# Gate product moved ahead of the inner products and the states in each slot of a state-space loop

## The chip, the core and the metric
The kernel runs on one core of one Trainium2 chip. The metric is the device time of one execution in microseconds (us). All times of the profile are from one profiled execution of the kernel before, counted from the start of its span.

## What is computed
Four layers one after the other on an input of 2 x 512 x 512: an attention layer, a gated feed-forward layer, a state-space layer (Mamba-2 style) and a grouped feed-forward layer, each with layer norms and a residual sum. The change is in the state-space layer, which works on 2 sequences of 512 positions, 128 heads of 64, in 8 groups of 16 heads, with chunks of 128 positions:

```python
proj = jnp.einsum('bsd,ed->bse', x, in_proj_w)
gate, hBC, dt = ...
hBC = jax.nn.silu(causal_conv4(hBC))            # per channel, 4 taps
Y_diag = einsum('bzlhn,bzshn,bhzls,bzshp->bzlhp', Cc, Bc, L, xch)    # inside a chunk
states = einsum('bzlhn,bhzl,bzlhp->bzhpn', Bc, decay_states, xch)    # a chunk's end state
Y_off  = einsum('bzlhn,bzhpn,bhzl->bzlhp', Cc, prev, exp(A_cum))     # from earlier chunks
y = Y_diag + Y_off + hs * D
g = y * jax.nn.silu(gate)
out = rmsnorm_per_group(g) * norm_w
return einsum('bsi,oi->bso', out, out_proj_w)
```

## The kernel before
The large products are in fp32r: each operand is cut into a high and a low part and three products are summed (`product`, L96 to L98), so 12 matmuls of 512 columns make one product over 512 inputs.

The state-space stage runs over 8 groups `g`, 2 sequences `b`, and `CT` = 10 slots `k` for each pair of these: 16 half-groups of 10 slots, and a tail. In the text, slot 7 means a slot with `k == 7`, and T7 the moment in which TensorE starts its conv product. The first two columns of a half-group are B and C, the other eight (`GT` = 8) are pairs of heads. A slot is a software pipeline: each engine has its own program of all slots, written out in order, and `behind(g, b, k, lag)` says which item a step with this lag works on (or none). What each engine does in a slot:

- TensorE (`on_tensor`): `projection` (the conv product, 12 matmuls), `inside` (lag 5, the products inside chunks, L1301), `states` (lag 5, L1310), `gate` (lag 3, the gate product, 12 matmuls), `project` (lag 8, output projection, 12 matmuls, L1331 to L1333), `before` (lag 6, the part of earlier chunks, L1344), in slot 6 `squares`, then `turn` (lag 4, transposes, L1356). Because of the lags, slots 3 and 4 have no `inside` and `states`, slots 1 and 2 no `gate`, slots 6 and 7 no `project`, slots 4 and 5 no `before`.
- VectorE (`on_vector`): first tap of the conv (`tap` 0), `with_dt` (xdt, L1521, waits for `turn` of the slot ahead), tap 1, `offset` (L1540), tap 2, `mixing` of one head (mix, L1547), `skip` (y, L1566, waits for `inside` of this slot), in slot 8 `accumulate` 0 and 1 (x, L1603), `carry` (state, L1572 and L1580, waits for `states` of this slot), `mixing` of the other head, in slot 8 `accumulate` 2 and 3, `low` (y_lo, L1588), and in the first sequence's half-groups `cut_out` (w_o_lo, L1593), once or twice a slot from slot 3 to slot 8. The three taps read the result of the last slot's conv product out of PSUM.
- ScalarE (`on_scalar`): weight cuts, the conv's first read (`first_tap`), SiLUs, `gate` (sg, L1451, which empties the gate product's bank), and the decays of mix. GpSimd (`on_pool`): `to_end` (xend), `finish` (y), low parts of weights, squares. SyncE issues all DMAs.

Two PSUM banks serve conv and gate products by turns, `k % 2` for the conv product and the other for the gate product. So the gate product of slot `k` overwrites the conv product of slot `k - 1`, and waits until its taps are done; the next conv product waits until ScalarE has emptied the gate's bank. One bank (`SPARE_D`) serves `inside` and `before` by turns, one (`SPARE_C`) `states` and `turn`, so that `before` and `turn` wait for `skip` and `carry` of the same slot:

```python
def gate(bb, i):
    wait(pe, "taps_done", g, b, (K1 - 1) * k if main else 0)
def before(bb, i):
    if i < GT - 1:
        wait(pe, "skip_done", g, bb, i + 2)
def turn(bb, i):
        wait(pe, "state_done", g, bb, 2 * i)
def project(bb, i):
        if i == 0:
            wait(pe, "acc_done", g, bb, z + 1 - ZB)
```

The last one holds in slot 8, where `project` starts a new accumulation in the four output banks that `accumulate` of the same slot empties.

Of the kernel before, what the change touches and what calls it, by code (L numbers as in the profile page):

```python
# [92 lines left out]
def product(pe, out, terms):  # L93

    for n, (a_hi, a_lo, b_hi, b_lo) in enumerate(terms):
        pe.matmul(out, a_hi, b_hi, start=(n == 0), stop=False)  # L96
        pe.matmul(out, a_hi, b_lo, start=False, stop=False)  # L97
        last = pe.matmul(out, a_lo, b_hi, start=False, stop=(n == len(terms) - 1))  # L98
    return last
# [800 lines left out]
def state_space(core, w_conv_in, w_gate_in, w_dt, w_out1, chan_wb, dt_bias, a_log, norm_w, c_keep):  # L900
# [8 lines left out]
    with ExitStack() as outer:  # L909
# [195 lines left out]
        with ExitStack() as inner:  # L1105
# [63 lines left out]
            def wait(eng, name, g, b, j):  # L1169

                value = (g * B + b) * PER[name] + j
                if value > 0:
                    eng.wait_ge(s[name], value)

            def behind(g, b, k, lag):

                i = k - lag
                if i >= 0:
                    return (b, i) if i < GT and g < G1 else (b, None)
                if g == 0 and b == 0:  # L1180
                    return b, None
                return (b - 1, i + CT) if i + CT < GT else (b - 1, None)
# [90 lines left out]
            def on_tensor(pe, g, b, k):  # L1273
# [3 lines left out]
                def projection():  # L1277
                    n = (b * CT + k) % RING
                    wait(pe, "win_low", g, b, k + 1)
                    wait(pe, "taps_done", g, b, (K1 - 1) * (k - 1))  # L1280
                    bb, i = behind(g, b, k, 4)
                    if i is not None:
                        wait(pe, "gate_done", g, bb, i + 1)
                    at = slice(b * S, (b + 1) * S)
                    last = product(pe, ps[:, k % 2, :], [
                        (w_in_hi[:, n, c, :], w_in_lo[:, n, c, :], xt_hi[:, c, at], xt_lo[:, c, at]) for c in range(KD)])
                    last.then_inc(s["proj_ready"], 1)
# [17 lines left out]
                def states(bb, i):  # L1305

                    wait(pe, "bt_done", g, bb, 1)
                    wait(pe, "xend_done", g, bb, i + 1)
                    for z in range(ZB - 1):
                        last = pe.matmul(ps[:, SPARE_C, cols(z)], bt[:, z, :], xend[:, i % 2, z, :], start=True, stop=True)  # L1310
                    last.then_inc(s["st_ready"], 1)

                def gate(bb, i):

                    wait(pe, "wg_low", g, bb, i + 1)
                    wait(pe, "taps_done", g, b, (K1 - 1) * k if main else 0)
                    at = slice(bb % B * S, (bb % B + 1) * S)
                    last = product(pe, ps[:, 1 - k % 2, :], [
                        (w_g_hi[:, i % RING, c, :], w_g_lo[:, i % RING, c, :], xt_hi[:, c, at], xt_lo[:, c, at]) for c in range(KD)])
                    last.then_inc(s["gate_ready"], 1)  # L1320
# [63 lines left out]

                if main:
                    projection()
                bb, i = behind(g, b, k, 5)
                if i is not None:
                    inside(bb, i)
                    states(bb, i)  # L1390
                bb, i = behind(g, b, k, 3)
                if i is not None:
                    gate(bb, i)
                bb, i = behind(g, b, k, 8)
                if i is not None:
                    project(bb, i)
                bb, i = behind(g, b, k, 6)
# [4 lines left out]
                bb, i = behind(g, b, k, 4)  # L1402
# [323 lines left out]
            with nc.Block() as blk:  # L1726
                @blk.sync
                def _(sp):
                    sp.dma_start(keep_ls[:, :], c_keep).then_inc(s["const_loaded"], 16)
                    groups(sp, loads)  # L1730

                @blk.tensor
                def _(pe):
                    pe.wait_ge(s["ones_set"], 1)
                    groups(pe, on_tensor)

                @blk.scalar
                def _(act):
                    groups(act, on_scalar)

                @blk.vector
                def _(dve):
                    dve.wait_ge(s["const_loaded"], 16)
                    groups(dve, on_vector)

                @blk.gpsimd
                def _(pool):
                    pool.memset(ones[:, :], 1.0).then_inc(s["ones_set"], 1)
                    pool.memset(acc[:, :, :], 0.0).then_inc(s["acc_zero"], 1)
                    groups(pool, on_pool)  # L1750
# [427 lines left out]
```

## Time and profile before
| | |
|---|---|
| time, median of 3 runs | 2871.81 us (2871.59 to 2872.53) |
| profiled execution: its time, its span | 2870.13 us, 2868.3 us |
| TensorE matmul busy over the span | 2618.6 us, 91% |
| VectorE, ScalarE, GpSimd busy over the span | 59%, 49%, 51% |
| mean granted TensorE clock | 0.964 |
| a light slot 8 (1667.64 to 1679.19), a heavy one (1771.73 to 1784.26) | 11.55 us, 12.53 us |
| TensorE busy in 1200 to 2600 us | 193 to 194 us in each 200 us |

The state-space loop runs from about 1090 us to about 2750 us. Its half-groups differ little from each other: two of them (one for each sequence) take 204.9 to 206.7 us in the steady part. Slots take 8.5 to 12.5 us. In the rows below, the half-group whose slot 0 starts at 1690.49 belongs to the first sequence (with `cut_out`, "heavy" in the text), the one ahead of it to the second ("light").

### The profile page before, as it was taken

What the parts mean: (1) busy time and instruction counts of PE and PEld (TensorE: products, weight loads), DVE (VectorE), ACT (ScalarE), POOL (GpSimd) and SP (SyncE); (2) the same over time, 40 slices, a digit from 0 to 9 for tenths busy, and PEclk for the clock granted to TensorE, in tenths of its full rate; (3) what the DMA queues carried; (4) which work ended last, traced back from release to release, by engine and by line L of the source; (5) the groups of instructions that cost most, each with busy time, mean ns of one, the idle gap of its engine ahead of it and who ended that gap; (6) DMA issues with size and microseconds to landing.
All of it is one profiled execution on the core that took longest, in us unless ns stands there. A gap on an engine that the chain in (4) does not pass through costs nothing. (4 is left out here: it accounts for less than half of the span.)

```text
span 2868.3 us, 37544 instructions
## 1 busy us (share of the span) xinstructions
PE 2618.6 (91%) x12920; PEld 1874.7 (65%) x12920; DVE 1680.8 (59%) x3054; ACT 1398.2 (49%) x2762; POOL 1457.5 (51%) x1267
## 2 busy tenths in 40 slices
PE   7999999799979936999999999999999999999948
PEld 3464444444458724787887887877877877877734
DVE  2131211366542464777777787678678778778765
ACT  2100000355322116677668668667766766866703
POOL 0042222344300103776776776786776776777651
PEclk9999999899989958999999999999999999999978
DMA  5000200000021015334334334333433333334210
GB/s 207 0 12 0 88 0 0 30 1 1 1 88 37 1 53 176 111 93 155 94 95 147 110 104 125 109 111 116 127 103 118 115 111 111 115 112 124 75 47 30
DMA packets 137292, 233.36 MB, mean 81 GB/s; under 512 B 27408, under 2 KB 47632, under 8 KB 136848
## 3 DMA queue, kind: packets, MB, share of 16 engines
q1 hardware_dynamic: 137104, 230.96, 25.7%
q8 instruction: 105, 1.72, 0.3%
q14 instruction: 83, 0.68, 0.1%
HBM read 223.57 MB, written 7.34 MB: 81 GB/s over the span
## 5 line engine op out<-in xcount | busy, mean ns | idle before, releaser
L428 PE MATMUL ps<-w,q 128*128 128x512 f32 x768 | 332.3, 592 | 1.5 <-DVE raw L449 1.5
L1459 ACT ACTIVATE mix<-mix,sc 128x128 f32<-128x128 f32 x1024 | 310.8, 389 | 3.4 <-DMA mix<-row_cum 3.3
L96 PE MATMUL ps<-s_xt_hi,w_in_hi 128*128 128x512 f32 x640 | 266.3, 416 | 49.0 <-ACT sg L1451 32.8
L1558 DVE SCALAR_TENSOR_TENSOR feat<-ps,chan,feat 128x511 f32<-128x511 f32 (+2 forms) x384 | 283.7, 739 | 10.4 <-ACT feat L1441 8.7
L1670 POOL TENSOR_TENSOR w_in_lo<-w_in_raw,w_in_hi 128x512 fp32r<-128x512 f32 x160 | 216.1, 1351 | 115.4 <-ACT w_in_hi L1416 115.4
L1547 DVE TENSOR_TENSOR mix<-mix,cb 128x512 f32<-128x512 f32 x256 | 271.7, 1066 | 0.0
L428 PEld LDWEIGHTS ps<-w,q 128*128 128x128 f32 x768 | 145.8, 190 | 185.1 <-issue 183.2
L1588 DVE TENSOR_TENSOR y_lo<-y,y_hi 128x512 fp32r<-128x512 f32 x128 | 171.0, 1336 | 161.0 <-ACT y_hi L1475 159.3
L98 PE MATMUL ps<-s_xt_hi,w_in_lo 128*128 128x512 f32 x640 | 252.4, 394 | 0.0
L97 PE MATMUL ps<-s_xt_lo,w_in_hi 128*128 128x512 f32 x640 | 251.1, 392 | 0.0
L1654 POOL TENSOR_TENSOR xend<-xdt,sc 128x384 f32<-128x384 f32 x128 | 106.8, 834 | 281.3 <-DVE xdt L1521 279.6
L96 PE MATMUL ps<-s_xt_hi,w_g_hi 128*128 128x512 f32 x512 | 213.2, 416 | 21.1 <-DVE feat L1558 21.0
L1331 PE MATMUL ps<-w_o_hi,y_hi 128*128 128x512 f32 x512 | 207.4, 405 | 5.4 <-DVE y_lo L1588 3.4
L502 POOL TENSOR_TENSOR sq<-raw 128x512 f32<-128x512 f32 (+1 forms) x24 | 23.2, 967 | 357.1 <-DVE raw L449 357.1
L98 PE MATMUL ps<-s_xt_hi,w_g_lo 128*128 128x512 f32 x512 | 204.0, 398 | 0.0
L1333 PE MATMUL ps<-w_o_hi,y_lo 128*128 128x512 f32 x512 | 203.3, 397 | 0.0
L1332 PE MATMUL ps<-w_o_lo,y_hi 128*128 128x512 f32 x512 | 203.1, 397 | 0.0
L97 PE MATMUL ps<-s_xt_lo,w_g_hi 128*128 128x512 f32 x512 | 201.5, 394 | 0.0
L1666 POOL TENSOR_TENSOR y<-y,sg 128x512 f32<-128x512 f32 x128 | 195.1, 1524 | 10.0
L1675 POOL TENSOR_TENSOR w_g_lo<-w_g_raw,w_g_hi 128x512 fp32r<-128x512 f32 x128 | 200.1, 1563 | 0.0
L653 ACT ACTIVATE qt<-ps 128x512 f32<-128x512 f32 x16 | 9.4, 665 | 381.6 <-PE ps L581 381.6
L1441 ACT ACTIVATE feat<-ps,chan 128x512 f32<-128x512 f32 x128 | 98.4, 769 | 180.6 <-PE ps L98 180.6
(246 smaller groups left out, 6006.3 us busy)
## 6 DMA issues: line engine op xcount, KB each, us to landing
mix<-row_cum SPq DMA_DIRECT2D x128, 512.0 KB, 5.7
w_in_raw<-in_w_conv_in SPq DMA_DIRECT2D x160, 256.0 KB, 3.3
w_g_raw<-in_w_gate_in SPq DMA_DIRECT2D x128, 256.0 KB, 3.4
ecb<-row_ecum SPq DMA_DIRECT2D x256, 96.0 KB, 3.4
w_o_raw<-in_w_out SPq DMA_DIRECT2D x64, 256.0 KB, 3.0
w<-in_w_c2q SPq DMA_DIRECT2D x16, 768.0 KB, 7.7
wqkv<-in_w_qkv SPq DMA_DIRECT2D x1, 3072.0 KB, 13.7
f_w_int<-in_w_gate SPq DMA_DIRECT2D x11, 256.0 KB, 2.6
```

The costliest lines, as they stand in the source:

```text
L96: pe.matmul(out, a_hi, b_hi, start=(n == 0), stop=False)
L97: pe.matmul(out, a_hi, b_lo, start=False, stop=False)
L98: last = pe.matmul(out, a_lo, b_hi, start=False, stop=(n == len(terms) - 1))
L428: mm = pe.matmul(dst, src[:, c, b, z * P + tap:(z + 1) * P + tap], w, start=(c == 0 and tap == 0), stop=False)
L1331: pe.matmul(ps[:, OUT + z, :], a_hi, w_o_hi[:, i, :], start=(i == 0), stop=False)
L1332: pe.matmul(ps[:, OUT + z, :], a_hi, w_o_lo[:, i, :], start=False, stop=False)
L1333: last = pe.matmul(ps[:, OUT + z, :], a_lo, w_o_hi[:, i, :], start=False, stop=(i == GT - 1))
L1459: last = act.activation(m, m, ACT.Relu, bias=sc[:, b, CUM, z, 2 * i + e:2 * i + e + 1], scale=-1.0)
L1547: last = dve.tensor_tensor(m, m, cb[:, :], ALU.mult)
L1558: dve.scalar_tensor_tensor(out=to, in0=ps[:, j % 2, 0:S - back], scalar=chan[:, bb % B, j, K1 - 1 - back:K1 - back], in1=to, op0=ALU.mult, ...
L1670: pool.tensor_tensor(w_in_lo[:, n % RING, :, :], w_in_raw[:, n % RING, :, :], w_in_hi[:, n % RING, :, :].bitcast(F32), ALU.subtract).then_ ...
L1675: pool.tensor_tensor(w_g_lo[:, i % RING, :, :], w_g_raw[:, i % RING, :, :], w_g_hi[:, i % RING, :, :].bitcast(F32), ALU.subtract).then_inc ...
```

## The change
In every slot TensorE's program has `gate` directly behind `projection`, ahead of `inside` and `states`. No instruction is added or removed, no wait is added or dropped, and the programs of the four other queues are word for word the same.

```diff
                 if main:
                     projection()
+                bb, i = behind(g, b, k, 3)
+                if i is not None:
+                    gate(bb, i)
                 bb, i = behind(g, b, k, 5)
                 if i is not None:
                     inside(bb, i)
                     states(bb, i)
-                bb, i = behind(g, b, k, 3)
-                if i is not None:
-                    gate(bb, i)
                 bb, i = behind(g, b, k, 8)
                 if i is not None:
                     project(bb, i)
```

TensorE's rows in a slot 7, before: from the last matmul of the conv product (w_in) over `inside` (mix, xdt), `states` (xend, bt) and the gate product (w_g) to `before` (featc, state) and `turn` (ident).

```order
L98 MATMUL ps<-s_xt_hi,w_in_lo 128x512
L1301 MATMUL ps<-mix,xdt 64x128 x8
L1310 MATMUL ps<-xend,bt 128x128 x3
L96 MATMUL ps<-s_xt_hi,w_g_hi 128x512
...
L98 MATMUL ps<-s_xt_hi,w_g_lo 128x512
L1344 MATMUL ps<-featc,state 128x128 x3
L1356 MATMUL ps<-ident,feat 128x128 x4
```

The same slot of the changed kernel:

```order
L98 MATMUL ps<-s_xt_hi,w_in_lo 128x512
L96 MATMUL ps<-s_xt_hi,w_g_hi 128x512
...
L98 MATMUL ps<-s_xt_hi,w_g_lo 128x512
L1301 MATMUL ps<-mix,xdt 64x128 x8
L1310 MATMUL ps<-xend,bt 128x128 x3
L1344 MATMUL ps<-featc,state 128x128 x3
L1356 MATMUL ps<-ident,feat 128x128 x4
```

The twelve matmuls of the gate product no longer stand between `states` and `before`; these two, and `inside` and `before`, are now neighbours.

TensorE's rows in a slot 8, before, which has the output projection (w_o) too:

```order
L98 MATMUL ps<-s_xt_hi,w_in_lo 128x512
L1301 MATMUL ps<-mix,xdt 64x128 x8
L1310 MATMUL ps<-xend,bt 128x128 x3
L96 MATMUL ps<-s_xt_hi,w_g_hi 128x512
...
L98 MATMUL ps<-s_xt_hi,w_g_lo 128x512
L1331 MATMUL ps<-w_o_hi,y_hi 128x512
...
L1344 MATMUL ps<-featc,state 128x128 x3
```

And in the changed kernel:

```order
L98 MATMUL ps<-s_xt_hi,w_in_lo 128x512
L96 MATMUL ps<-s_xt_hi,w_g_hi 128x512
...
L98 MATMUL ps<-s_xt_hi,w_g_lo 128x512
L1301 MATMUL ps<-mix,xdt 64x128 x8
L1310 MATMUL ps<-xend,bt 128x128 x3
L1331 MATMUL ps<-w_o_hi,y_hi 128x512
...
L1344 MATMUL ps<-featc,state 128x128 x3
```

Here `inside` and `states` stand between the gate product and the output projection, and the gate product follows the conv product at once. The same exchange is made in slots 0, 5, 6, 7, 8 and 9; slots 1 to 4 keep their order, since they lack one of the two.

## Rows read from the trace of the kernel before

**Rows 1.** What TensorE waited for, 1200 to 2600 us: total, times, longest.

```profile
PE ps L96 <- DVE feat L1558: 20.7, 14, 2.7
PE ps L96 <- ACT sg L1451: 20.3, 21, 1.3
PE ps L1331 <- DVE x L1603: 1.7, 6, 0.3
```

**Rows 2.** Timeline of TensorE, slot 0: start, us, instruction, [idle before].

```profile
1690.49 0.47 PE L96 MATMUL ps<-s_xt_hi,w_in_hi 128*128 128x512 f32 x1
...
1693.43 1.10 PE L1301 MATMUL ps<-mix,xdt 128*64 128x128 f32 x16
...
1695.15 0.47 PE L96 MATMUL ps<-s_xt_hi,w_g_hi 128*128 128x512 f32 x1
...
1698.00 0.39 PE L1331 MATMUL ps<-w_o_hi,y_hi 128*128 128x512 f32 x1
...
1700.80 0.83 PE L1344 MATMUL ps<-featc,state 128*128 128x128 f32 x6
1701.46 0.60 PE L1356 MATMUL ps<-ident,feat 128*128 128x128 f32 x4
1701.82 0.48 PE L96 MATMUL ps<-s_xt_hi,w_in_hi 128*128 128x512 f32 x1
```

**Rows 3.** Timeline of VectorE, the same slot 0.

```profile
1690.78 0.69 DVE L1521 TENSOR_TENSOR xdt<-ps,sc 128x512 f32<-128x512 f32 x1 [2.52 <-PE ps L1356]
...
1692.50 0.74 DVE L1558 SCALAR_TENSOR_TENSOR feat<-ps,chan,feat 128x509 f32<-128x509 f32 x1
...
1694.58 0.75 DVE L1566 SCALAR_TENSOR_TENSOR y<-feat,chan,ps 128x512 f32<-128x512 f32 x1 [0.35 <-PE ps L1301]
...
1696.53 0.68 DVE L1547 TENSOR_TENSOR mix<-mix,cb 128x512 f32<-128x512 f32 x1
1697.13 1.53 DVE L1588 TENSOR_TENSOR y_lo<-y,y_hi 128x512 fp32r<-128x512 f32 x1
1698.58 0.74 DVE L1558 SCALAR_TENSOR_TENSOR featb<-ps,chan,featb 128x511 f32<-128x511 f32 x1
```

**Rows 4.** Timeline, slot 4 of a light half-group: last tap, gate product.

```profile
1631.40 0.73 DVE L1558 SCALAR_TENSOR_TENSOR feat<-ps,chan,feat 128x509 f32<-128x509 f32 x1
...
1632.28 0.47 PE L96 MATMUL ps<-s_xt_hi,w_g_hi 128*128 128x512 f32 x1 [0.28 <-DVE feat L1558]
```

**Rows 5.** Timeline of VectorE, light slots 7 and 8.

```profile
1664.30 1.70 DVE L1547 TENSOR_TENSOR mix<-mix,cb 128x512 f32<-128x512 f32 x1
1667.05 0.69 DVE L1588 TENSOR_TENSOR y_lo<-y,y_hi 128x512 fp32r<-128x512 f32 x1 [1.05 <-ACT y_hi L1475]
...
1672.35 1.40 DVE L1603 SCALAR_TENSOR_TENSOR x<-ps,rr,x 128x512 f32<-128x512 f32 x2
...
...
1675.87 1.40 DVE L1603 SCALAR_TENSOR_TENSOR x<-ps,rr,x 128x512 f32<-128x512 f32 x2
```

**Rows 6.** Timelines of ScalarE (slot 6) and TensorE (slots 7, 8), light.

```profile
1656.60 0.60 ACT L1451 ACTIVATE sg<-ps 128x512 f32<-128x512 f32 x1 [1.02 <-PE ps L98]
...
1666.45 0.60 PE L1356 MATMUL ps<-ident,feat 128*128 128x128 f32 x4
1667.64 0.47 PE L96 MATMUL ps<-s_xt_hi,w_in_hi 128*128 128x512 f32 x1 [0.60 <-ACT sg L1451]
```

**Rows 7.** Timeline, heavy slot 5: the last two taps, `inside`.

```profile
1744.30 1.51 DVE L1558 SCALAR_TENSOR_TENSOR feat<-ps,chan,feat 128x510 f32<-128x510 f32 x2
...
1744.65 1.09 PE L1301 MATMUL ps<-mix,xdt 128*64 128x128 f32 x16
```

**Rows 8.** Group of `cut_out`, 1200 to 2600 us: busy, mean ns, idle before.

```profile
L1593 DVE SCALAR_TENSOR_TENSOR w_o_lo<-w_o_raw,nw,w_o_hi 128x512 fp32r<-128x512 f32 x55 | 66.0, 1220 | 0.0
```

**Rows 9.** Windows over two heavy gate products: us, busy by engine, PEclk, DMA.

```profile
1735.70:1739.00 3.30, 3.27 (x14) 2.73 (x15) 3.15 (x3) 1.81 (x5) 3.22 (x3) 1.00 0.03 9
2147.30:2151.80 4.50, 4.45 (x13) 3.57 (x14) 4.35 (x4) 3.03 (x9) 4.42 (x4) 0.65 0.03 9
```

## The prediction
> **What bounds the kernel now.** I read the page first (TensorE 91% busy, the others near half), then the list of waits of the state-space loop, then the timelines of TensorE and VectorE slot by slot. In 1400 us of the loop TensorE waits about 43 us: 20.7 for taps, 20.3 for ScalarE's sg, 1.7 for the accumulations [rows 1]. So TensorE is the bound, and nothing done to the order of its work can give back more than these 3%. What counts is whether VectorE, which shares PSUM banks with it, still delivers in time once its partners on TensorE move.
>
> In a full slot TensorE issues without a gap [rows 2]. From T (start of the conv product): `inside` and `states` at +2.94, gate product +4.66, `project` +7.51, `before` +10.31, `turn` +10.97, next slot +11.33. So the pieces hold it 2.9 (conv or gate), 1.72, 2.80 (`project`), 0.66 and 0.36.
>
> VectorE in the same slot [rows 3]: xdt at +0.29 (0.29 behind the end of `turn`), last tap ending at +2.75, y at +4.09, which is 1.15 behind the start of `inside`; then, counted from y: the second mix at 1.95 (so `carry` is done near 2.05), y_lo at 2.55, next slot's first tap at 4.00, done at 4.74. That is +8.83, and xdt is due at 11.33 + 0.29 = 11.62: VectorE has 2.8 us to spare, seen as its 2.52 us wait for `turn`.
>
> **The change, part by part.** It adds and removes nothing. It starts the gate product 1.7 us earlier, and `inside`, `states` 2.9 later. Nothing else moves, DMA issues included.
>
> *The gate product's own wait.* It waits for the last tap of the same slot. In a slot 4, where nothing stands between the products, a tap that ended at 1632.13 let the gate go at 1632.28, 0.15 later [rows 4]. A punctual VectorE ends its taps at +2.75, so the gate can go at +2.90, as TensorE comes free. Cost 0 to 0.05 us, but the cover of 1.7 us is gone: from here on each microsecond of lateness of VectorE costs TensorE one.
>
> *VectorE's loop.* `inside` is now at +5.80, y at +6.95, taps done at 11.69, xdt due at 11.62. The spare 2.8 us are used up: in full slots (9 and 0) it fits to 0.1 us. In shorter slots and where VectorE has more to do it does not. Slot by slot, light half-groups first:
>
> - Slot 5: no `offset`, taps early. 0.
> - Slot 6: no `project` between `states` and `before` any more. `before` waits for y: 6.95 + 0.75 + 0.15 = +7.85 against +7.5. 0.35. `squares` covers the wait of `turn`.
> - Slot 7: the same 0.35; then `turn` waits for `carry`: 6.95 + 2.05 + 0.15 = +9.15 against 8.2 + 0.35 = 8.5, so 0.65 more. Its gate product meets taps 0.4 late, since slot 6 was 9.7 long and VectorE's loop 11.4 less what slot 7 leaves out. Given back: ScalarE's sg. It waited 1.02 us for the gate product of slot 6 and so came late in slot 7, where conv 8 waited for it: 1667.64 less 1666.45 + 0.36 is 0.83 [rows 6]. The gate product now is done before ScalarE comes to it, so this goes. Sum 0.35 + 0.65 + 0.4 - 0.83 = +0.6.
> - Slot 8: y of slot 7 is at T7 + 7.35, the second mix at 9.3. It took 1.70 in the old place, 0.68 in slot 0; y_lo 0.69 and 1.53 [rows 3, 5]. Where they fall beside GpSimd's work is not known; I take 1.1 and 1.0, between the bounds. With the first tap, xdt starts at T7 + 12.0. Slot 7 is now 9.9 long (8.5 + 1.0 + 0.4), so this is T8 + 2.05 and 1.75 late; the gate product is 1.7 late. Then `inside` at +7.5, y at 8.65, accumulations 0 and 1 from 9.3 to 10.7. `project` comes at +9.2 (7.5 + 1.7) and waits for accumulation 0 until 10.15 (0.95). Accumulations 2 and 3 start 3.52 behind 0 and 1 [rows 5], at 12.85, so `project`'s third bank, due at 11.55, waits until 13.65 (2.1). The old slot lost 0.25 here (of the 1.7 us of x [rows 1]). Sum 1.7 + 0.95 + 2.1 - 0.25 = 4.5.
> - Slots 9 and 0: 0.1 together.
>
> Light: 0.35 + 0.6 + 4.5 + 0.1 = 5.5 us.
>
> Heavy half-groups have w_o_lo besides, 1.22 us each [rows 8], one in each of slots 5 to 8 and two in slots 3 and 4. In slot 5 the last taps end at 1745.81, so the gate could go at 1745.96, while `inside` took over from conv at 1744.65 [rows 7]: 1.3, now paid in full. Slots 6 and 7: 0.5 each. Slot 8: xdt 1.2 later than in the light one, so gate 2.9 late, then 0.95 and 2.1, in all 5.9; the old heavy slot already lost 1.2 by the same late VectorE (12.53 against 11.33 for a full slot). 4.7. Slot 9: 0.3. Heavy: 7.3 us.
>
> Eight light half-groups give 44. Seven heavy ones give 51; the first half-group has no accumulation and is held by ScalarE, 0. Together 95 us.
>
> *TensorE's clock.* After a 2.7 us wait for taps in a heavy slot 4, one gate product ran at granted 1.00 and took 3.3 us, another at 0.65 and took 4.5 [rows 9]: part of the latter was at 1.2 instead of 2.4 GHz, 1.2 us dearer, for a like wait ahead of it. The Trainium skill (TensorE: Matmul & The Clock Gate, Part 1) has idleness bring the half rate; the trace agrees, with 0.65, though not each time. The new waits of slot 8 are of this size. I count 1.2 us in half of 15 slots 8: 9 us; bounds 0 and 2.4 x 15 = 36.
>
> Sum: 2870.1 (the profiled execution, 1.7 below the median) + 95 + 9 = **2974 us**, +3.6%, and 2976 by the median.
>
> **Rivals.**
>
> *Faster: VectorE keeps up in slot 8.* Then the change only removes ScalarE's waits: 0.83 in each light half-group and the like of it in heavy ones (20.3 us in seven pairs, of which slot 4's stay): 8 x 2 = 15 us, 2856. It decides at xdt of slot 8 starting by T8 + 0.4. For it: the sg wait that goes is real. Against it: even with both shared operations at their short 0.69, xdt comes at T7 + 11.2, which is T8 + 1.4. 4%. No measurable change, by such a balance: 3%.
>
> *Half the cost.* Second mix and y_lo take 0.69 wherever VectorE comes late, because GpSimd has by then finished. Then the light slot 8 costs 3.2, slots 6 and 7 nothing, heavy ones 4.5 in all: 8 x 3.2 + 7 x 4.5 = 57, 2927. For it: GpSimd runs while VectorE waits for `inside`. Against it: GpSimd's chain in slot 7 starts with xdt, which is late too. 15%.
>
> *VectorE becomes the bound in every slot from 5 to 0.* The loop fits full slots to 0.1 us only with y_lo and mix as in slot 0. If they take 1.53 and 1.70 there, the loop is 12.4 against 11.33 in two slots, and slots 7 and 8 are dearer by 1: some 3 us more in each half-group, 48, and the clock at its upper bound, 27 more: 2974 + 75 = 3049. For it: both long values are in the rows. Against it: the total work of VectorE is as before, and the collisions so far fall where GpSimd is busiest. Beside it, the Trainium skill (SBUF — State Buffer, Who interferes with whom) says that VectorE and GpSimd hold a shared port by turns, for a whole instruction. The trace agrees in the two lengths of y_lo, 0.69 and 1.53. 16%.
>
> **The numbers.** Main case 62%, its own range 2940 to 3010. Half cost 15%, VectorE bound 16%, faster 4%, same 3%. The range for 8 in 10 reaches into both neighbours: 2920 to 3035. A measurement tells 0.2% (6 us) from no change. Slower: 0.93, same 0.03, faster 0.04.
>
> **What the new profile would show.** TensorE's wait for taps (L96 behind L1558) grows from 20.7 us to over 60 in the same 1400 us, with over 30 entries. New lines: `before` waiting for y (L1344 behind L1566), about 0.3 each in slots 6 and 7, and `turn` for state (L1356 behind L1580). The wait of L1331 for x grows from 1.7 to some 30 us. The wait for sg falls, to what slot 4 has. VectorE no longer waits for L1356 before xdt but for L1301 before y, some 3 us a slot. A light slot 8 grows from 11.55 to 16. If slot 8 starts its gate product at +2.9, the prediction is wrong; if it is late but `project` does not wait for accumulations, it is too high by half.

## The result: 2.5% slower

The changed kernel takes 2944.81 us (median of 4 runs, 2943.51 to 2947.16) against 2871.7 us (4 runs of the kernel before, 2869.87 to 2872.53) on the same chip: a ratio of 1.0254, 95% interval 1.024 to 1.0268, or 73 us. Its profiled execution took 2943.51 us, with a span of 2941.7.

The list of waits of TensorE in the changed kernel, 1200 to 2600 us, answers to [rows 1]:

```profile
PE ps L96 <- DVE feat L1558: 41.3, 32, 2.7
PE ps L1331 <- DVE x L1603: 26.4, 26, 1.3
PE ps L96 <- ACT sg L1451: 6.5, 6, 1.2
PE ps L1356 <- DVE state L1580: 5.0, 13, 0.4
```

The waits for taps doubled, from 20.7. The wait for the accumulations (x), 1.7 before, is now 26.4 in 26 entries, that is two in each of 13 slots 8. `turn` waits for `carry`, as it never did. The wait for sg fell from 20.3. Together 79 us against 46. The 46 hold one more row of the list of the kernel before, the wait of `inside` for off, which is in neither [rows 1] nor the prediction's 43 us, and which has gone:

```profile
PE ps L1301 <- DVE off L1540: 3.7, 6, 0.6
```

Where it happens is seen in the timeline of TensorE in a light slot 7's end, slot 8 and the start of slot 9; it answers to [rows 6]:

```profile
1692.93 0.63 PE L1356 MATMUL ps<-ident,feat 128*128 128x128 f32 x4 [0.38 <-DVE state L1580]
1693.32 0.47 PE L96 MATMUL ps<-s_xt_hi,w_in_hi 128*128 128x512 f32 x1
...
1697.46 0.47 PE L96 MATMUL ps<-s_xt_hi,w_g_hi 128*128 128x512 f32 x1 [1.13 <-DVE feat L1558]
...
1700.39 1.09 PE L1301 MATMUL ps<-mix,xdt 128*64 128x128 f32 x16
...
1703.09 0.47 PE L1331 MATMUL ps<-w_o_hi,y_hi 128*128 128x512 f32 x1 [0.74 <-DVE x L1603]
...
1706.00 0.50 PE L1331 MATMUL ps<-w_o_hi,y_hi 128*128 128x512 f32 x1 [1.30 <-DVE x L1603]
...
1708.51 0.48 PE L96 MATMUL ps<-s_xt_hi,w_in_hi 128*128 128x512 f32 x1
```

Slot 8 is 15.19 us long here, was 11.55. Three waits in a row: for the last tap, for accumulation 0, for accumulation 2. VectorE in the same stretch answers to [rows 3, 5]:

```profile
1690.75 0.75 DVE L1566 SCALAR_TENSOR_TENSOR y<-feat,chan,ps 128x512 f32<-128x512 f32 x1 [3.23 <-PE ps L1301]
...
1692.70 0.97 DVE L1547 TENSOR_TENSOR mix<-mix,cb 128x512 f32<-128x512 f32 x1
1693.60 0.68 DVE L1588 TENSOR_TENSOR y_lo<-y,y_hi 128x512 fp32r<-128x512 f32 x1
...
1694.86 0.67 DVE L1521 TENSOR_TENSOR xdt<-ps,sc 128x512 f32<-128x512 f32 x1
...
1696.58 0.73 DVE L1558 SCALAR_TENSOR_TENSOR feat<-ps,chan,feat 128x509 f32<-128x509 f32 x1
...
1701.53 0.75 DVE L1566 SCALAR_TENSOR_TENSOR y<-feat,chan,ps 128x512 f32<-128x512 f32 x1 [3.25 <-PE ps L1301]
1702.19 1.40 DVE L1603 SCALAR_TENSOR_TENSOR x<-ps,rr,x 128x512 f32<-128x512 f32 x2
...
1704.60 0.69 DVE L1547 TENSOR_TENSOR mix<-mix,cb 128x512 f32<-128x512 f32 x1
1705.21 1.40 DVE L1603 SCALAR_TENSOR_TENSOR x<-ps,rr,x 128x512 f32<-128x512 f32 x2
```

VectorE waits 3.2 us for `inside` ahead of each y, and is late at the next slot's taps, since it can start the rest of its slot only then: xdt starts 1.54 behind T8, where 0.29 is punctual. The second mix and y_lo, however, took 0.97 and 0.68, near their short lengths.

The length of each kind of slot, as the median distance between the first matmuls of two conv products in the steady part of the timelines (us):

| slot | 4 | 5 | 6 | 7 | 8 | 9 | 0 |
|---|---|---|---|---|---|---|---|
| light, before | 9.27 | 10.63 | 9.38 | 9.38 | 11.55 | 11.31 | 11.33 |
| light, changed | 9.26 | 10.57 | 9.64 | 9.69 | 15.22 | 11.42 | 11.44 |
| heavy, before | 13.09 | 10.64 | 9.37 | 9.99 | 12.52 | 11.31 | 11.33 |
| heavy, changed | 13.20 | 10.60 | 9.62 | 10.35 | 15.85 | 11.43 | 11.44 |

Slots 1 to 3 are unchanged to 0.01. Slot 8 has 3.67 and 3.33 us of the 4.41 and 4.83 by which mean light and heavy half-groups grew. One row hides a part: a heavy slot 4 of the kernel before took 11.62 to 11.64 us in three of seven half-groups and 13.08 to 13.29 in four (so slots are not all within the 12.5 us named ahead), and 13.19 to 13.29 in all seven of the changed kernel.

### The profile page after: what moved, and what is told of

Same layout as the page of the kernel before. It is cut to its first block and busy times, and to the rows that moved or that the text cites. A ratio compares the mean times of both kernels' runs of the same rounds, so it can differ in the third digit from the quotient of the medians.

```text
span 2941.7 us, 37544 instructions
## 1 busy us (share of the span) xinstructions
PE 2642.7 (90%) x12920; PEld 1875.6 (64%) x12920; DVE 1612.2 (55%) x3054; ACT 1397.0 (47%) x2762; POOL 1403.1 (48%) x1267
## 3 DMA queue, kind: packets, MB, share of 16 engines
q8 instruction: 105, 1.72, 0.2%
## 5 line engine op out<-in xcount | busy, mean ns | idle before, releaser
L1566 DVE SCALAR_TENSOR_TENSOR y<-feat,chan,ps 128x512 f32<-128x512 f32 x128 | 95.6, 747 | 343.5 <-PE ps L1301 343.5
L1547 DVE TENSOR_TENSOR mix<-mix,cb 128x512 f32<-128x512 f32 x256 | 253.6, 995 | 0.0
L1588 DVE TENSOR_TENSOR y_lo<-y,y_hi 128x512 fp32r<-128x512 f32 x128 | 128.9, 1007 | 134.1 <-ACT y_hi L1475 132.3
```

Of the source, the lines that this page charges most:

```text
L1547: last = dve.tensor_tensor(m, m, cb[:, :], ALU.mult)
```

## Experiments

### One group of slots at a time
`on_tensor` got a flag that says in which slots the gate product stands first:

```diff
+                first = k != 8        # k == 8; k in (6, 7); k in (5, 9, 0)
+                bb, i = behind(g, b, k, 3)
+                if i is not None and first:
+                    gate(bb, i)
                 bb, i = behind(g, b, k, 5)
                 if i is not None:
                     inside(bb, i)
                     states(bb, i)
                 bb, i = behind(g, b, k, 3)
-                if i is not None:
+                if i is not None and not first:
                     gate(bb, i)
```

All but slot 8. 

> The gate product stands first in slots 5, 6, 7, 9 and 0, and in its old place in slot 8. Theory A (VectorE, handed on late from slots 6 and 7, meets the gate product without cover in slot 8, and the accumulations behind it hold the output projection): nearly all of the loss sits in slot 8, so this one is within 15 us of the kernel before, 2872 to 2890 us; TensorE's waits for x (L1331 behind L1603) fall from 2.0 us in a slot 8 to under 1.2. Theory B (every exchanged slot costs a little, the wait of the gate product for its taps): 5 of 6 exchanged slots stay, so some 60 of the 73 us stay, 2930 us.

Slot 8 alone. 

> The gate product stands first in slot 8 alone. Theory A: slot 8 receives a VectorE that is as early as before (xdt at T8 + 0.68 in a light half-group, + 1.66 in a heavy one), so the gate product waits 0.4 and 1.3 us, less than now (1.13 and 1.82), but the accumulations still hold the projection by 2.0 us: about +2.3 us in each of 15 slots 8, 2900 to 2912 us. Theory B: one slot of six, 12 us, 2884. Theory C (slot 8 alone is the whole loss, whatever the slots ahead do): 2945.

Slots 6 and 7 alone. 

> The gate product stands first in slots 6 and 7 alone. Theory A: the wait of turn for the states (0.39 a slot 7) and the gate product's wait in heavy ones are paid for by the removed wait for sg (0.83 in light and more in heavy half-groups); slot 8 keeps its cover. Within 10 us of the kernel before, 2862 to 2882. Theory B: two slots of six, 24 us more, 2896.

Slots 5, 9 and 0 alone. 

> The gate product stands first in slots 5, 9 and 0 alone. Theory A: full slots fit the loop of VectorE, and slot 5 has early taps, so 0 to 12 us more, 2872 to 2884 (in a heavy slot 9, VectorE comes late out of slot 8 and the gate product could wait up to 1 us). Theory B: three slots of six, 36 us more, 2908. If A holds, the excess of this one, of slots 6 and 7 alone and of slot 8 alone add up to less than the 73 us of the whole change, since lateness handed from slot 7 to slot 8 is in none of them; if the costs are each slot's own, they add up to 73.

| gate product first in | time, us | ratio to before (95%) | slots 7 + 8, light | slots 7 + 8, heavy |
|---|---|---|---|---|
| no slot (before) | 2871.0 | | 9.38 + 11.55 | 9.99 + 12.52 |
| all but 8 | 2908.01 | 1.0131 (1.0114 to 1.0147) | 9.66 + 12.45 | 10.34 + 13.09 |
| 8 | 2920.33 | 1.0169 (1.0153 to 1.0184) | 9.38 + 14.34 | 9.99 + 15.32 |
| 6, 7 | 2893.92 | 1.0082 (1.0067 to 1.0097) | 9.67 + 12.45 | 10.34 + 13.08 |
| 5, 9, 0 | 2883.02 | 1.0044 (1.0029 to 1.0059) | 9.38 + 11.57 | 9.99 + 12.53 |

Theory A fell in part. All but slot 8 leaves 37 us, where A gave at most 19. Slot 8 alone costs 49 us, more than A's 29 to 41, and slots 6 and 7 alone 23, where A gave at most 11. Only slots 5, 9 and 0, with 12 us, lie where A had them. The three parts sum to 49 + 23 + 12 = 84, where A wanted less than 73. Theories B and C fell too: all but slot 8 costs 37 us and not some 60, and slot 8 alone is neither a sixth nor the whole.

Of the 11 us by which the parts exceed the whole, 4 are found in heavy slots 9. With the old slot 8, VectorE comes late out of it, the gate product of slot 9 waits 0.44 us, and slot 9 takes 11.94 instead of 11.31; with the new slot 8 it takes 11.43. The rest is not split up.

The columns say where. A light slot 8 grows by 2.79 if it is exchanged itself, by 0.90 if slots 6 and 7 are, and by 3.67 if both are: the two add. The 2.79 are in every slot 8 with the new order, late VectorE or not. The timeline of TensorE in a light slot 8 with that slot alone exchanged:

```profile
1685.30 0.47 PE L96 MATMUL ps<-s_xt_hi,w_g_hi 128*128 128x512 f32 x1 [0.27 <-DVE feat L1562]
...
1690.91 0.47 PE L1331 MATMUL ps<-w_o_hi,y_hi 128*128 128x512 f32 x1 [0.74 <-DVE x L1607]
```

The wait for taps is only 0.27, but that for x is 0.74 as in the full change (lines are 4 higher here), and the next one for x 1.30. Since y, accumulations and `project` all follow `inside`, which now stands directly ahead of `project`, these waits don't depend on how punctual VectorE was. And the 0.90 handed on by slot 7 is paid even where slot 8 has the old order, since there `inside` waits for off, which VectorE computes between the taps. TensorE's waits with all but slot 8 exchanged:

```profile
PE ps L96 <- DVE feat L1562: 30.2, 28, 2.7
PE ps L1301 <- DVE off L1544: 10.5, 13, 1.2
...
PE ps L1331 <- DVE x L1607: 3.7, 13, 0.3
```

10.5 us in 13 entries, where the kernel before has 3.7 in 6. The 1.7 us that stood between the conv and gate products cover the taps, but not off. In a heavy slot 8 this wait is 1.16 to 1.19 us.

### VectorE's order, changed to fit
Accumulations first:

```diff
+                if later and k == 8:
+                    for z in range(ZB):
+                        accumulate(b - 1, z)
                 if i5 is not None:
                     skip(bb5, i5)
-                if later and k == 8:
-                    accumulate(b - 1, 0)
-                    accumulate(b - 1, 1)
...
-                if later and k == 8:
-                    accumulate(b - 1, 2)
-                    accumulate(b - 1, 3)
```

> The changed kernel, and in slot 8 VectorE makes its four accumulations ahead of y, in the time in which it waits for inside. If the price of slot 8 is mostly the output projection held by the accumulations (waits of 0.74 and 1.30 us in each), L1331's waits for x go, slot 8 falls by about 2.3 us from 15.2 and 15.9, and the time by 15 x 2.3 = 35 us to 2910. If these waits only stand in for a later one (y, and with it carry, is put off by what does not fit before inside), slot 8 hardly gets shorter: above 2935.

Taps first, in all slots:

```diff
                 if j is not None:
                     tap(bbc, j, 0)
+                    tap(bbc, j, 1)
+                    tap(bbc, j, 2)
                 if main and k == 4:
                     mask()
                 if i5 is not None:
                     with_dt(bb5, i5)
-                if j is not None:
-                    tap(bbc, j, 1)
                 if later and k == 7:
                     mean(b - 1)
                 if i7 is not None:
                     offset(bb7, i7)
-                if j is not None:
-                    tap(bbc, j, 2)
```

> The changed kernel, and in every slot VectorE makes the three taps one after the other, ahead of xdt, mean and off. If the gate product's wait is the lost cover of VectorE's chain ahead of the last tap, the wait for taps falls by 1.1 us in each late slot 8 and by 0.7 in heavy slots 7, and more in slot 4: some 5 us in a pair of half-groups, 38 in all, 2907 us; L96's wait for taps in 1200 to 2600 us falls from 41 to under 15 us. If the lateness is only moved on to xdt and inside, a new wait of L1301 for xdt takes its place and the time stays above 2935.

Both edits. 

> The changed kernel with both edits of VectorE's order. If the two waits (for taps, for the accumulations) are the price of the change, this one loses both, 35 + 38 us, and is back at 2872, within 12 us of the kernel before; what stays is 0.6 us a half-group of slots 6 and 7. If not, it stays well above 2900.

Both edits on the kernel before. 

> The kernel before (gate product behind the states) with both edits of VectorE's order. If the exchange of the gate product is worth nothing even where VectorE is in time, this one is faster than the changed kernel with both edits, by up to 10 us; it gains on the kernel before by the wait for taps in slot 4 (2.66 and 0.28 us a pair), by the waits for off and x in heavy slots 8 (1.2), and by the clock behind them: 20 to 35 us, 2836 to 2851. If the exchange has a gain of its own, the removed wait for sg, that other kernel is the faster by up to 10 us.

| kernel | time, us | ratio to before (95%) | slot 8 light, heavy |
|---|---|---|---|
| before | 2870.61 | | 11.55, 12.52 |
| changed, accumulations first | 2912.81 | 1.0151 (1.0136 to 1.0166) | 12.69, 14.89 |
| changed, taps first | 3005.87 | 1.0476 (1.0457 to 1.0495) | 16.19, 17.22 |
| changed, both | 2967.68 | 1.0341 (1.0323 to 1.0359) | 13.34, 15.77 |
| before, both | 2941.88 | 1.0255 (1.0239 to 1.0272) | 12.58, 12.81 |

*Accumulations first* leaves 42 of the 73 us, so it gave back 31, with 35 expected. VectorE makes all four while it waits for `inside`, and the waits for x are gone. That part of the price is shown. A light slot 8 lost 2.53 us. A heavy one lost only 0.96 in the median, but the seven are of two kinds: three took 13.34 to 13.37 us and so lost 2.5 like the light ones, four took 14.89 to 14.92. The missing 1.5 us of these four is the clock. The gate product of a heavy slot 8 starts after a like wait in both kernels. The timeline of TensorE with accumulations first:

```profile
1797.04 0.47 PE L96 MATMUL ps<-s_xt_hi,w_g_hi 128*128 128x512 f32 x1 [1.83 <-DVE feat L1558]
...
1801.32 1.28 PE L1301 MATMUL ps<-mix,xdt 128*64 128x128 f32 x16
```

The window over this gate product (the column behind POOL is the granted clock), with accumulations first:

```profile
1797.00:1801.40 4.40, 4.36 (x14) 3.06 (x16) 3.50 (x5) 2.90 (x9) 4.32 (x4) 0.65 0.19 68
```

And in the changed kernel, the same product of the same half-group, its row of the timeline and its window:

```profile
1808.22 0.47 PE L96 MATMUL ps<-s_xt_hi,w_g_hi 128*128 128x512 f32 x1 [1.82 <-DVE feat L1558]
```

```profile
1808.20:1811.30 3.10, 3.08 (x14) 2.31 (x16) 0.84 (x1) 1.62 (x4) 3.02 (x3) 1.00 0.28 100
```

*Taps first* made the kernel dearer, by 62 us on top of the change, where 38 less were expected: this expectation failed altogether. The waits of TensorE in that kernel:

```profile
PE ps L96 <- DVE feat L1558: 43.5, 24, 2.9
PE ps L96 <- ACT sg L1451: 30.3, 22, 2.1
PE ps L1331 <- DVE x L1603: 27.8, 24, 1.7
PE ps L1301 <- DVE off L1540: 19.5, 26, 1.2
```

The wait for taps did not even fall, those for off and sg grew. xdt and off come later, and with them the two chains that start from them on GpSimd: xend, and y, which ScalarE and then VectorE (y_lo) wait for (ScalarE's wait for GpSimd's y in 1200 to 2600 us grew from 53.1 to 168.7 us). Most of the new loss is not in slot 8: of the 4.2 us by which a light half-group grew beyond the changed kernel, 3.7 are in slots 1 to 4, which the exchange does not touch.

Both edits together failed likewise, 2967.68 us where 2872 was expected. And on the kernel before they cost 71 us where a gain of 20 to 35 was expected, so the taps-first edit is dear whatever the order of the products. That kernel is 26 us faster than the changed one with both edits: the exchange is not a gain of its own here either. To see the taps near slot 8 alone, the edit was limited.

### Taps first in slots 7 and 8 only
The kernel with the accumulations first, and in slots 7 and 8 the order tap 0, tap 1, tap 2, xdt, mean, off.

> The changed kernel with the four accumulations ahead of y, and with the taps ahead of xdt, mean and off in slots 7 and 8 alone (in all slots it put off off, and with it inside, in slots 1 and 2). If VectorE's lateness at the last tap is what is left of the price, the wait for taps goes in light slots 8 (1.13 us) and heavy slots 7 (0.7), and falls from 1.83 to about 0.7 in heavy slots 8, and with so short a wait TensorE keeps its full clock there (the gate product falls from 4.35 to 3.0 us long): light slot 8 from 12.7 to 11.6, heavy one from 14.9 to 12.4, 2885 us. If the same lateness returns as a wait of inside for off or xdt, 2905 or more.

It took 2931.34 us, ratio 1.0212 (1.0192 to 1.0231): 59 us above the kernel before, where 42 stood without the edit, so 17 dearer. Slot 7 fell as expected (heavy 10.34 to 9.44), but slot 8 grew (12.69 to 13.32, and 14.89 to 15.88, medians), and so did slot 9 (11.44 to 11.84, and 11.45 to 12.26). The expectation gave 2885, or 2905 and more if the lateness came back as a wait of `inside`. The time lies in the second range, but the lateness came back elsewhere, as a wait for taps: 57.5 us in 1200 to 2600 us, 43.6 without the edit. The timeline of VectorE from a heavy slot 7 to slot 8 shows where:

```profile
1795.11 0.90 DVE L1547 TENSOR_TENSOR mix<-mix,cb 128x512 f32<-128x512 f32 x1
1795.92 1.78 DVE L1588 TENSOR_TENSOR y_lo<-y,y_hi 128x512 fp32r<-128x512 f32 x1
1797.63 1.52 DVE L1593 SCALAR_TENSOR_TENSOR w_o_lo<-w_o_raw,nw,w_o_hi 128x512 fp32r<-128x512 f32 x1
1799.08 2.30 DVE L1558 SCALAR_TENSOR_TENSOR feat<-ps,chan,feat 128x511 f32<-128x511 f32 x3
```

And GpSimd at the same time:

```profile
1795.40 1.75 POOL L1676 TENSOR_TENSOR w_g_lo<-w_g_raw,w_g_hi 128x512 fp32r<-128x512 f32 x1
1797.12 1.49 POOL L1684 TENSOR_TENSOR y_sq_sum<-y 128x512 f32<-128x512 f32 x1
```

y_lo took 1.78 and w_o_lo 1.52, instead of 0.68 and 0.74 in the changed kernel. y_lo ends 0.55 behind w_g_lo. The Trainium skill (SBUF — State Buffer, Who interferes with whom) says that the ports which the two engines share are locked for one of them, and that the other is blocked until that instruction is over. The trace agrees with 1.78 against 0.68 for one instruction. GpSimd's chain, put off by the later off, reaches into the stretch in which VectorE has mix, y_lo and w_o_lo. The three taps in a row took 2.30 us, where they took 3.11 with xdt and off between them: 0.8 us won. But they start 3.36 us behind T8 instead of 1.55: 1.8 us lost ahead of them. So the wait for taps in that heavy slot 8 rose from 1.83 to 2.82.

### Does the exchange pay anywhere?


> The kernel before with the accumulations ahead of y. In the old order they hold the projection by 0.25 us in a light slot 8 and some 0.5 in a heavy one, so this is worth 3 to 6 us at most: 2864 to 2871. A gain like the 32 us that the same edit gave the changed kernel would mean that the accumulations are a bottleneck of their own, whatever the order of the products.

> The gate product first in slot 6 alone. It lets ScalarE go on up to 1 us earlier, so that the conv product of slot 8 no longer waits for sg (0.83 us in a light half-group, more in a heavy one), and costs the wait of before for y, 0.26, in slot 6. If the removed wait for sg is a real gain: slot 7 falls from 9.38 and 9.99 to about 8.6 and 8.9, 8 to 14 us less, 2857 to 2863. If the lateness of VectorE grows by what TensorE gains, the inside of slot 8 waits for off instead, and the time is within 3 us of before.

> The same with the accumulations ahead of y in slot 8. If both are gains of their own, they add up: 2852 to 2860 us, faster than both kernels.

| kernel | time, us | ratio to before (95%) | slots 7 + 8, light | heavy |
|---|---|---|---|---|
| before | 2872.14 | | 9.38 + 11.55 | 9.99 + 12.52 |
| before, accumulations first | 2869.8 | 0.9992 (0.9982 to 1.0002) | 9.38 + 11.32 | 9.99 + 11.98 |
| slot 6 only | 2882.46 | 1.0033 (1.0021 to 1.0045) | 8.52 + 12.46 | 8.76 + 13.09 |
| slot 6 only, accumulations first | 2872.75 | 1.0005 (0.9994 to 1.0016) | 8.51 + 11.91 | 8.87 + 12.83 |

The old order with the accumulations first came out as expected. The two kernels with slot 6 exchanged did not: slot 6 only is 10 us dearer, where a gain of 8 to 14 or no more than 3 us either way was expected, and with the accumulations first it is level with the kernel before, where 12 to 20 us less were expected.

With slot 6 alone exchanged the wait for sg goes as forecast: slot 7 is 0.86 and 1.23 us shorter. But slot 8 is 0.91 and 0.57 longer and slot 6 by 0.26. The medians hide that three of seven heavy slots 8 took 14.0 to 15.1 us instead of 13.1, and that six of seven heavy slots 4 took over 13.0, where four did before. The timeline of TensorE in a light slot 8 of that kernel:

```profile
1678.43 1.09 PE L1301 MATMUL ps<-mix,xdt 128*64 128x128 f32 x16 [0.55 <-DVE off L1544]
...
1684.85 0.50 PE L1331 MATMUL ps<-w_o_hi,y_hi 128*128 128x512 f32 x1 [0.28 <-DVE x L1607]
```

and of VectorE just ahead:

```profile
1672.41 1.81 DVE L1551 TENSOR_TENSOR mix<-mix,cb 128x512 f32<-128x512 f32 x1
1674.15 1.76 DVE L1592 TENSOR_TENSOR y_lo<-y,y_hi 128x512 fp32r<-128x512 f32 x1
1675.83 0.74 DVE L1562 SCALAR_TENSOR_TENSOR feat<-ps,chan,feat 128x511 f32<-128x511 f32 x1
```

and of GpSimd beside it:

```profile
1673.63 1.72 POOL L1679 TENSOR_TENSOR w_g_lo<-w_g_raw,w_g_hi 128x512 fp32r<-128x512 f32 x1
```

TensorE arrives sooner, VectorE does not, and the wait for sg has become one for off. In the kernel before, y_lo of a light slot 7 waited 1.05 us for ScalarE's y_hi and then took 0.69 [rows 5]. Here it has nothing to wait for and starts 1.03 us sooner behind T7, but now beside w_g_lo, and takes 1.76. It ends 9.51 us behind T7, where it ended 9.47 behind. So the 0.83 us that ScalarE held up TensorE gave nothing: what VectorE gained by the earlier start went into one longer operation. No version tried beats the kernel before beyond what can be measured; the old order with the accumulations first is level with it.

## Why the prediction was right, and where its sizes were off

The direction, the place (slot 8) and the mechanism (VectorE's loop, whose spare 2.8 us are used up) held; 2945 lies in the range of 2920 to 3035, and the forecast of 2974 had +104 where +73 was measured. The waits for taps came to 41.3 us where over 60 were forecast, those for x to 26.4 where 30 were.

- **The gate product's own wait.** Small, as forecast: in slots 9 and 0, with a punctual VectorE, 0.11 us each, where 0.1 together was forecast.
- **Slots 6 and 7.** Mechanism right but for one name: forecast 0.95 light and 1.0 heavy, measured 0.57 (0.26 + 0.31) and 0.61. `turn` waits for `carry`, with 0.38 idle instead of 0.65. `before` does start after y (0.26), but it shows in no entry of the list, since the idle time left behind the modelled end of `states` is 0.08 us (1691.57 to 1691.65 in a light slot 7). The sg wait goes, as counted.
- **Slot 8.** The mis-sized term. Light: forecast 4.5 = 1.7 + 0.95 + 2.1 - 0.25, measured 3.67. The idle times of 1.13, 0.74 and 1.30 count from the modelled end of the matmul ahead; from start to start the gate product comes 1.20 late (1697.46 less 1693.32 is 4.14, against 2.94), `project` 0.98 (2.70 behind `inside`, against 1.72), and `project` takes 1.60 longer (4.40, against 2.80). So 0.95 was right, and 1.7 and 2.1 were too large by 0.5 each. The step that was off is "I take 1.1 and 1.0": mix took 0.97 and y_lo 0.68, and in slot 8 the second mix took the short 0.69 instead of the 1.20 that the distance of 3.52 between the accumulations held; it was 3.02. Heavy: forecast 4.7, measured 3.33, for the same reason: the gate product was 1.87 late instead of 2.9, with mix 0.97, y_lo 0.68 and w_o_lo 0.74. The rival "half the cost" named the cause, and lay too low in the time.
- **Why the short lengths.** VectorE waits 3.2 us for `inside`, and GpSimd goes on in that time. Its last operation of the light slot 7 shown above:

```profile
1692.10 1.03 POOL L1683 TENSOR_TENSOR y_sq_sum<-y 128x512 f32<-128x512 f32 x1
```

  It ends 0.47 us ahead of y_lo at 1693.60. In the changed kernel y_lo's mean fell from 1359 ns and w_g_lo's on GpSimd from 1575 ns to those of this list of groups (1200 to 2600 us; busy, mean ns, idle before):

```profile
L1675 POOL TENSOR_TENSOR w_g_lo<-w_g_raw,w_g_hi 128x512 fp32r<-128x512 f32 x104 | 145.3, 1397 | 0.0
...
L1588 DVE TENSOR_TENSOR y_lo<-y,y_hi 128x512 fp32r<-128x512 f32 x105 | 107.2, 1021 | 110.1 <-ACT y_hi L1475 108.6
```

  The limited taps-first kernel shows the reverse.
- **Slot 5, heavy.** Forecast 1.3, measured nothing (10.64 to 10.60). Its late taps were read in a half-group whose slot 4 ran at full clock. In the profile after, the gate product of slot 4 is slowed in all seven heavy half-groups (4.5 us long), in the one before in four of seven. A slowed slot 4 gives VectorE 1.5 us to catch up. The kernels with slot 5 exchanged show both cases. All but slot 8, slots 5, 9 and 0, accumulations first, and the limited taps-first kernel have seven heavy slots 4 at full clock between them (11.6 to 11.7 us), and behind each the gate product of slot 5 waits 1.22 to 1.27 us and the slot takes 12.06 to 12.12. Behind every slowed one it takes 10.6 to 10.7. TensorE in slot 5 of one of the seven (all but slot 8):

```profile
1763.16 0.47 PE L96 MATMUL ps<-s_xt_hi,w_g_hi 128*128 128x512 f32 x1 [1.25 <-DVE feat L1562]
```

  So the forecast wait of 1.3 is right where slot 4 runs at full clock, and the step that failed is to count it in all seven. Slots 4 and 5 together take 23.8 us in either case, against 22.3 before at full clock.
- **The clock in slot 8.** Counted 9 us, measured none there; the accumulations-first kernel has it in four of seven heavy slots 8. In slot 4 there are three more slowed products, with slots 1.6 us longer, 5 us in all in the profiled execution. Whether the exchange brings them is not shown: in the profiles of the kernels that leave slot 4's taps alone, three to seven of seven heavy slots 4 are slowed.
- **The sum.** 8 light half-groups by 4.41 (forecast 5.5) and 7 heavy ones by 4.83 (forecast 7.3) give 69. The first half-group took 2.2 more, where the forecast had 0. The stage began 2.6 later, at 1093.7, which is chance: in the profiles of the experiments it begins anywhere from 1091.2 to 1095.0. What follows the loop gives back 0.6: 73.
- **A reason that did not hold.** That the removed sg wait is worth 0.83 a half-group as such. In the slot 6 kernel it was worth nothing, since y_lo, freed of its wait for ScalarE, grew from 0.69 to 1.76 and VectorE was no earlier at slot 8. And lateness handed to slot 8 is paid in either order, so the lost cover accounts for less of slot 8 than was thought; 2.5 of its 3.7 us, which the accumulations-first kernel gave back, are the direct succession of `inside` and `project`, with y and the accumulations between them on VectorE.

## What to carry to other kernels
When a producer is moved later in one engine's order, list every consumer on the other engines that stands between it and the next instruction here; what was cover for them (the 12 matmuls of the gate product between `states` and `project`) was worth 31 of the 73 us, as moving the accumulations showed. A wait of the busiest engine is worth its length only if no other late engine stands right behind it: trace what each removed wait would meet next. And the length of an operation like y_lo, which took 0.68 to 1.78 us by what GpSimd did beside it, belongs to its place in time, so a reordering that looks free on one queue changes lengths on the others.

## What was not expected of the hardware
- One VectorE subtraction of 128x512 in fp32 took 0.68 to 1.78 us, by what GpSimd was doing (y_lo, 0.68 in the changed kernel's slots 7 and 8, 1.78 in the limited taps-first kernel).
- After idle times of 1.82 and 1.83 us ahead of the same gate product the granted clock was 1.00 in one kernel (the changed one) and 0.65 in the other (accumulations first). The length of a wait alone does not say whether the clock falls; what else decides is open.
